# The attention mask of a pooling step: penalties gathered from a table by the sequence's type, one addition in place of four masked products

## The chip, the cores and the metric

The kernel runs on one core of one Trainium2 chip. The metric is device time in microseconds (us) of one execution. The core has TensorE (PE), VectorE (DVE), ScalarE (ACT), GpSimd (POOL) and the sync engine's queue (SP), which issues most of the DMAs.

## The reference, cut to what matters

Four residual layers are applied to `x` of 16 sequences x 256 positions x 256 channels, all in float32. Layer 0 has sixteen exponential moving averages and a layer norm. Layer 1 is the pooling that the change touches. Layer 2 is a mixture of eight experts and a shared one, computed for every sequence, and layer 3 a two-layer head whose last 64 output columns come from an expert chosen by the sequence.

```
attn_in = tanh(hidden @ W1 + b1);  scores = attn_in @ v            # one score for each key l
mask = where(pt == 0, l <= j, where(pt == 1, l >= j, l != j))      # pt: type of the sequence, 0, 1 or 2
p = softmax(where(mask, scores[:, None, :], -1e30), axis=-1)       # 256 rows j, 256 keys l
cnt = sum(mask, -1)
x = x + einsum('bjl,bld->bjd', p, hidden) / cnt[..., None]
```

The type is an input, one integer for each of the 16 sequences.

## The kernel before, in words

**Work.** The 16 sequences form eight blocks of two. Each sequence of a block is a lane `s` (0 or 1). Layers 0 and 1 of a lane are cut into 47 side steps (`side(b, s, j)`, j = 0 to 46). Layers 2 and 3 of a block are a run of experts, each in eight chunks. One expert chunk of a whole block is twelve matmuls of 512 columns (`front`), an activation on ACT, a product on DVE (`hid`), a split of the result into a rounded high part on ACT and a low remainder on POOL (`hid_lo`, in `late`), and six matmuls into `ps_out` (`back`). Each matmul product is written as three, of high and low parts. The weights of a chunk are split likewise by ACT (`w_hi`) and DVE (`w_lo`) in `cut`. After the last chunk of an expert DVE adds `ps_out` into `acc` with the expert's coefficient, and the next expert's first `back` waits for it.

**Order.** Each engine runs its own share of one list, `ORDER`, made by the planner `order()` before the kernel is built. The side steps of blocks 1 to 7 are dealt out between the fronts. `side_cost(b, j)` gives each step a cost, and the lane with the smaller sum of costs goes next, lane 1 having started 12 units behind. After each front `pace(i) * step_budget(i - 1)` is added to a credit (capped at 6), and side steps are placed while it is positive. `pace` is the cost still to be placed for a block, over the budget that is left before the block's first front, and at most 1.1. A step that uses PE isn't placed behind a front if its lane has already had a step of non-zero cost there. If a block is due and its side steps are not all placed, the rest are placed at once, back to back (here called a join). The cost function before:

```
if 7 <= j < 7 + ND:
    return 2.1
...
return {0: 1.3, 5: 1.0, 34: 1.7, 36: 1.4, 39: 2.1, 42: 1.5, 24: 0.0, ...}.get(j, 0.7)
```

Block 0 has a written order: lane 0's steps, with some of lane 1's between them, come before the first front.

**Steps touched by the change.** Steps 8 to 23 have the sums of the averages on POOL (`add1` to `add15`), which add `trace[s][d % 3]` to `temporal[s]`. The third buffer, `trace[s][2]`, is last used by `add14`. Step 24 does nothing before. Step 39: PE multiplies by `v` so that the scores, the same in every partition, stand in PSUM; DVE (lines 1031, 1034, 1038) adds the penalties to them: `mask[:, 0]` (keys after the row) times `pen[:, 0, q]`, `mask[:, 1]` (keys before the row) times `pen[:, 1, q]`, and for each half of the rows the identity `idn` times `pen[:, 2, q]` on the diagonal. `pen` holds -1e30 or 0 for each sequence. Step 40 is the row maximum (1042) and its negation. Step 41 has transposes of the layer's input on PE (617), which overwrite the bank of the scores and so wait for the first of the four products (`sc0`), and the exponentials on ACT (817). Step 42 is the division on DVE (1056), 44 the transposes of the probabilities on PE (626), 46 the product.

POOL also gathers expert rows with an indirect DMA (line 1213): 128 rows of 512 floats for each sequence. `setup("route")` on POOL works out `typ`, `pen`, `cnt`, the coefficients and the row numbers for that gather.

Of the kernel before, what the change touches and what calls it, by code (L numbers as in the profile page):

```python
# [5 lines left out]
P = 128  # L6
B, S, D = 16, 256, 256
T = B * S
DH = D // P
BB = 2  # L10
BT = BB * S
NBLK = T // BT
ND = 16
# [38 lines left out]
NEG = -1e30  # L52
# [31 lines left out]
def side_cost(b, j):  # L84

    if 7 <= j < 7 + ND:
        return 2.1
    if b == 0 and j in (1, 26, 30, 32, 45):
        return 0.0
    return {0: 1.3, 5: 1.0, 34: 1.7, 36: 1.4, 39: 2.1, 42: 1.5, 24: 0.0, 25: 0.0, 29: 0.0, 37: 0.0, 43: 0.0}.get(j, 0.7)  # L90

# [14 lines left out]
def order():  # L106
# [126 lines left out]
    while queue:  # L233
# [11 lines left out]
            + [f"{what}{d}" for d in range(ND) for what in ("mul", "scan")]  # L245
            + ["t_lo", "prod", "p_lo", "q_lo", "rstd", "norm", "affine", "x1", "sc0", "sc1", "score",
               "max", "top", "xT_lo", "den", "rden", "prob", "probT_lo", "res"])
# [22 lines left out]

def residual_stack_kernel(nc, xT, chunks, head_chunks, sidew, vec128, w64, masks, ident, we_rows,
                          be_pad, blendT, taus, types, experts, gates, shared_gate, yT):
# [5 lines left out]
    with ctx:  # L278
# [68 lines left out]
        bn2_half = sb("bn2_half", [ND, 1])  # L347
        mask = sb("mask", [P, 2, 2, S], bf16)
        idn = sb("idn", [P, P])
# [11 lines left out]
        typ = sb("typ", [P, 5, B])  # L361
        pen = sb("pen", [P, 3, B])
        cnt = sb("cnt", [P, B, 2])
        ge = sb("ge", [P, B, NE])
# [21 lines left out]
        s_x = [[sem(f"x_in{s}_{i}") for i in range(2)] for s in range(BB)]  # L386
        s_we = [sem(f"we_in{i}") for i in range(2 * BB)]
        s_y = [sem(f"y_out{i}") for i in range(NACC)]

# [47 lines left out]
        def _(sp):  # L437
# [33 lines left out]
            sp.dma_start(wa1_t[:].rearrange("p k a -> p (k a)"), sidew[:, NSPLIT:NSPLIT + 2 * P]).then_inc(s_late, 16)  # L471
            sp.dma_start(mask[:].rearrange("p n j l -> p (n j l)"), masks.bitcast(bf16)).then_inc(s_late, 16)
            sp.dma_start(idn[:], ident[:]).then_inc(s_late, 16)
# [22 lines left out]
        def _(pe):  # L496
# [26 lines left out]
            def side(b, s, j):  # L523
# [79 lines left out]
                elif j == 38:  # L603
                    pe.wait_ge(l_dve[s], dve_at(s, b, "x1"))
                    pe.wait_ge(l_act[s], act_at(s, b, "std"))
                    if b == 0:
                        pe.wait_ge(s_late, 64)
                    plain_sum(ps[:, 0:S], [(wa1_t[:, k, :], temporal[s][:, k, :])
                                             for k in range(DH)]).then_inc(l_pe[s], 1)
                elif j == 39:  # L610
                    pe.wait_ge(l_act[s], act_at(s, b, "attn"))
                    mm(ps[:, 0:S], v_col.broadcast_to([P, P]), sm[:], start=True, stop=True).then_inc(l_pe[s], 1)
                elif j == 41:
                    pe.wait_ge(l_dve[s], dve_at(s, b, "sc0"))
                    for lh in range(2):
                        for dh in range(DH):
                            last = nc.tensor.transpose(ps[:, lh * D + dh * P:lh * D + (dh + 1) * P],
                                                       temporal[s][:, dh, lh * P:(lh + 1) * P], idn[:])
                    last.then_inc(l_pe[s], 1)
                elif j == 44:  # L620
                    pe.wait_ge(l_dve[s], dve_at(s, b, "prob"))
                    if b == 0:
                        pe.wait_ge(l_act[s], act_at(s, b, "xT"))
                    for jh in range(2):
                        for lh in range(2):
                            last = nc.tensor.transpose(ps[:, lh * S + jh * P:lh * S + (jh + 1) * P],  # L626
                                                       trace[s][1][:, jh, lh * P:(lh + 1) * P], idn[:])
                    last.then_inc(l_pe[s], 1)
                elif j == 46:
                    if b == 0:  # L630
                        pe.wait_ge(l_act[s], act_at(s, b, "probT"))
                    else:
                        pe.wait_ge(l_dve[s], dve_at(s, b, "probT_lo"))
                    for dh in range(DH):
                        c = slice(dh * P, (dh + 1) * P)
                        if b == 0:
                            last = plain_sum(both[:, dh, :], [(gated[s][:, lh, c], soma[s][:, lh, :]) for lh in range(2)])
                        else:
                            last = exact_sum(both[:, dh, :], [(one_hi[s][:, lh, c], one_lo[s][:, lh, c],
                                                               two_hi[s][:, lh, :], two_lo[s][:, lh, :]) for lh in range(2)])  # L640
                    last.then_inc(l_pe[s], 1)
# [68 lines left out]
            for x in ORDER:  # L710
# [4 lines left out]
                elif x[0] == "back":  # L715
                    (back_plain if x[1] < NLONE else back)(x[1])
                elif x == ("setup", "bias"):
                    pe.wait_ge(su_pool, su(SETUP_POOL, "onehot"))
                    pe.wait_ge(s_late, 64)
                    mm(ps_out[:, 0, 0:B], be_sb, onehot[:], start=True, stop=True).then_inc(su_pe, 1)  # L720
# [184 lines left out]
        def _(dve):  # L905
# [39 lines left out]
            def side(b, s, j):  # L945
# [80 lines left out]
                elif j == 39:  # L1026
                    if b == 0:
                        dve.wait_ge(su_pool, su(SETUP_POOL, "onehot"))
                        dve.wait_ge(s_late, 64)
                    dve.wait_ge(l_pe[s], pe_at(s, b, "score"))  # L1030
                    STT(score[:], mask[:, 0], pen[:, 0, q:q + 1],
                        ps[:, 0:S].unsqueeze(1).broadcast_to([P, 2, S]), ALU.mult, ALU.add).then_inc(l_dve[s], 1)
                    mine("sc0")
                    STT(score[:], mask[:, 1], pen[:, 1, q:q + 1], score[:], ALU.mult, ALU.add).then_inc(l_dve[s], 1)
                    mine("sc1")
                    for jh in range(2):
                        diagonal = score[:, jh, jh * P:(jh + 1) * P]
                        last = STT(diagonal, idn[:], pen[:, 2, q:q + 1], diagonal, ALU.mult, ALU.add)
                    last.then_inc(l_dve[s], 1)
                elif j == 40:  # L1040
# [118 lines left out]
        def _(pool):  # L1159
# [6 lines left out]
            def setup(j):  # L1166
# [8 lines left out]
                elif j == "route":  # L1175
# [10 lines left out]
                    done("cnt0")  # L1186
                    TS(pen[:], typ[:, 1:4, :], NEG, None, ALU.mult)
                    for jh in range(2):
# [4 lines left out]
                    done("cnt1")  # L1193
                    TT(cnt[:], parts[:, 0], parts[:, 1], ALU.add)
                    TS(sg[:, 1, :], sg[:, 0, :], -1.0, 1.0, ALU.mult, ALU.add).then_inc(su_pool, 1)
                    done("sg")
                    TT(cnt[:], cnt[:], parts[:, 2], ALU.add)
                    for e in range(NE):
                        TT(coef[:, e, :], ge[:, :, e], sg[:, 1, :], ALU.mult)
# [17 lines left out]
            def side(b, s, j):  # L1217
                if 9 <= j < 8 + ND:
                    d = j - 8
# [103 lines left out]
```

## Time and profile before

| | |
|---|---|
| median of 3 runs | 2991.48 us (2990.12 to 2994.9) |
| profiled execution | 2992.09 us |
| its span, first to last instruction | 2990.3 us (1.8 us lie around it) |
| mean granted TensorE clock | 0.979 |
| busy: PE / DVE / ACT / POOL | 2856.0 / 1782.0 / 1425.4 / 1169.9 us |

The busy time is the sum of an engine's instructions in the profiled execution. PE works for 96% of the span, so what can be won by a change to another engine is in the rest: the stretches in which PE waits. The granted clock is 1.00 at 2.4 GHz and 0.50 at 1.2 GHz.

### The profile page before, as it was taken

To read this page: it belongs to the slowest core of one execution; us is meant where nothing else is said; L and a number is where in the kernel's file an instruction comes from. 1 tells how busy PE (TensorE), PEld (TensorE's weight loads), DVE (VectorE), ACT (ScalarE), POOL (GpSimd) and SP (SyncE) were. 2 spreads that over 40 slices of the span, in tenths; PEclk is the share of its full clock that TensorE was granted. 3 is DMA by queue.
4 is the path that set the end of the run, shared out by engine and by line. 5 is a ranking of instruction groups with operands and counts; after the bars stand their busy time and mean duration, and the time that the engine had idled before them with its cause. 6 is when DMAs were issued, how large, how long until landed. Compare 5 with 4: busy or idle time off the path is not lost.

```text
span 2990.3 us, 37374 instructions
## 1 busy us (share of the span) xinstructions
PE 2856.0 (96%) x13486; PEld 2384.0 (80%) x13486; DVE 1782.0 (60%) x2922; ACT 1425.4 (48%) x2460; POOL 1169.9 (39%) x931
## 2 busy tenths in 40 slices
PE   5799999998999999998999999999899998999998
PEld 3588788887888888887888878888788887888887
DVE  7668776765665576656665467656455555333443
ACT  1244664464345563455434555347533446334544
POOL 4216334533443245433454235543334433333333
PEclk6899999999999999999999999999999999999999
DMA  2223231121111131112111112112111112111331
GB/s 100 92 90 94 79 103 43 53 78 43 50 51 44 45 89 60 48 37 87 49 43 43 46 44 84 43 43 70 55 43 53 51 48 77 60 48 45 115 99 39
DMA packets 75688, 185.87 MB, mean 62 GB/s; under 512 B 8936, under 2 KB 21744, under 8 KB 75504
## 3 DMA queue, kind: packets, MB, share of 16 engines
q1 hardware_dynamic: 73648, 179.17, 19.7%
q0 software_dynamic: 1280, 4.20, 0.4%
q8 instruction: 108, 1.77, 0.2%
q14 instruction: 76, 0.62, 0.1%
q10 hardware_dynamic: 576, 0.11, 0.0%
HBM read 179.25 MB, written 4.19 MB: 61 GB/s over the span
## 4 chain that ended last, share of the span: by engine, by line
PE 85%; DVE 8%; ACT 3%; issue 3%; DMA 0%; POOL 0%; DVEq 0%; ACTq 0%; SPq 0%
PE bank L508 18%; PE bank L510 18%; PE bank L509 18%; PE ps_out L508 9%; PE ps_out L510 9%; PE ps_out L509 9%; PE bank L501 3%; DVE w_lo L1076 2%; DVE trace L990 2%; DVE trace L998 1%; PE bank L578 1%; ACT w_hi L835 1%; PE ps_out L663 1%; DVE acc L1122 1%; PE bank L626 0%
## 5 line engine op out<-in xcount | busy, mean ns | idle before, releaser
L1229 POOL TENSOR_TENSOR hid_lo<-hid,hid_hi 128x512 fp32r<-128x512 f32 (+1 forms) x640 | 825.1, 1290 | 1638.4 <-ACT hid_hi L882 1638.1
L508 PE MATMUL bank<-res_lo,w_hi 128*128 128x512 f32 (+1 forms) x2432 | 950.4, 391 | 6.7 <-issue 3.9
L509 PE MATMUL bank<-res_hi,w_lo 128*128 128x512 f32 (+1 forms) x2432 | 938.1, 386 | 0.0
L510 PE MATMUL bank<-res_hi,w_hi 128*128 128x512 f32 (+1 forms) x2432 | 937.9, 386 | 0.0
L1105 DVE TENSOR_TENSOR hid<-hid,bank 128x512 f32<-128x512 f32 (+1 forms) x608 | 397.0, 653 | 628.9 <-PE bank L510 513.0
L872 ACT ACTIVATE hid<-bank 128x512 f32<-128x512 f32 (+1 forms) x608 | 349.7, 575 | 743.6 <-PE bank L510 666.3
L1076 DVE TENSOR_TENSOR w_lo<-w_raw,w_hi 128x768 fp32r<-128x768 f32 (+1 forms) x488 | 441.6, 905 | 385.6 <-ACT w_hi L835 310.0
L510 PEld LDWEIGHTS bank<-res_hi,w_hi 128*128 128x128 f32 x2432 | 458.8, 189 | 97.1
L508 PEld LDWEIGHTS bank<-res_lo,w_hi 128*128 128x128 f32 x2432 | 459.7, 189 | 95.6 <-issue 8.4
L835 ACT ACTIVATE w_hi<-w_raw 128x768 fp32r<-128x768 f32 x360 | 304.3, 845 | 466.0 <-PE ps_out L510 465.8
L509 PEld LDWEIGHTS bank<-res_hi,w_lo 128*128 128x128 f32 x2432 | 459.8, 189 | 81.6
L508 PE MATMUL ps_out<-hid_lo,w_hi 128*128 128x512 f32 (+1 forms) x1344 | 504.8, 376 | 13.5 <-DVE acc L1122 12.8
L510 PE MATMUL ps_out<-hid_hi,w_hi 128*128 128x512 f32 (+1 forms) x1344 | 503.9, 375 | 0.0
L509 PE MATMUL ps_out<-hid_hi,w_lo 128*128 128x512 f32 (+1 forms) x1344 | 503.7, 375 | 0.0
L882 ACT ACTIVATE hid_hi<-hid 128x512 fp32r<-128x512 f32 (+1 forms) x640 | 391.9, 612 | 11.1 <-DVE hid L1105 10.8
L1223 POOL TENSOR_TENSOR temporal<-temporal,trace 128x512 f32<-128x512 f32 x240 | 327.5, 1365 | 151.0 <-DVE trace L998 150.9
L998 DVE TENSOR_TENSOR_SCAN trace<-bank,trace 128x256 f32<-128x256 f32 x480 | 304.8, 677 | 8.2
L508 PEld LDWEIGHTS ps_out<-hid_lo,w_hi 128*128 128x128 f32 x1344 | 253.3, 188 | 66.8 <-issue 16.7
L509 PEld LDWEIGHTS ps_out<-hid_hi,w_lo 128*128 128x128 f32 x1344 | 253.7, 189 | 46.9
L510 PEld LDWEIGHTS ps_out<-hid_hi,w_hi 128*128 128x128 f32 x1344 | 253.7, 189 | 45.3
L990 DVE SCALAR_TENSOR_TENSOR trace<-gated,bl,bank 128x256 f32<-128x256 f32 x512 | 221.6, 474 | 57.6 <-PE bank L578 52.1
L578 PE MATMUL bank<-mod_pair,sel 128*128 128x256 f32 x256 | 82.5, 328 | 43.3 <-DVE trace L998 17.6
(178 smaller groups left out, 1952.9 us busy)
## 6 DMA issues: line engine op xcount, KB each, us to landing
w_raw<-in_chunks SPq DMA_DIRECT2D x360, 384.0 KB, 3.0
w_raw<-in_head_chunks SPq DMA_DIRECT2D x64, 224.0 KB, 2.5
plain<-in_chunks SPq DMA_DIRECT2D x32, 384.0 KB, 3.2
x_in<-in_xT SPq DMA_DIRECT2D x16, 256.0 KB, 3.4
out_yT<-acc SPq DMA_DIRECT2D x8, 512.0 KB, 3.1
acc<-in_sidew SPq DMA_DIRECT2D x2, 512.0 KB, 7.0
acc<-in_sidew SPq DMA_DIRECT2D x1, 320.0 KB, 5.4
mask<-in_masks SPq DMA_DIRECT2D x1, 256.0 KB
```

The source lines that it names most:

```text
L508: mm(out, wh, xl, start=start and i == 0, stop=False, skip_group_check=not lone)
L509: mm(out, wl, xh, start=False, stop=False, skip_group_check=not lone)
L510: last = mm(out, wh, xh, start=False, stop=end, skip_group_check=not lone)
L835: last = activate(w_hi[k][:], raw[:], ACT.Copy)
L872: activate(h[:, tok], ps_gate[i % 2][:, tok], ACT.Silu).then_inc(s_act, 1)
L882: activate(hid_hi[i % DEPTH][:, tok], hid[i % 3][:, tok], ACT.Copy).then_inc(s_hhi, 1)
L990: last = STT(tr[:, h, :], gated[s][:, h, :], bl[:, h, d:d + 1], (lead_mix[d % 2] if lead else ps)[:, 0:S], ALU.mult, ALU.mult)
L998: last = V.tensor_tensor_scan((temporal[s] if d == 0 else tr)[:, h, :], decay.broadcast_to([P, S]), tr[:, h, :], 0.0, ALU.mult, ALU.add)
L1076: return TT(w_lo[k][:, cols], src, f(w_hi[k][:, cols]), ALU.subtract)
L1105: TT(h[:, tok], h[:, tok], ps_up[i % 2][:, tok], ALU.mult).then_inc(s_hid, 1)
L1223: nc.gpsimd.tensor_tensor(temporal[s][:], temporal[s][:], trace[s][d % 3][:], ALU.add).then_inc(l_pool[s], 1)
L1229: nc.gpsimd.tensor_tensor(hid_lo[i % DEPTH][:, tok], hid[i % 3][:, tok], f(hid_hi[i % DEPTH][:, tok]), ALU.subtract).then_inc(s_hlo, 1)
```

## The change

The host makes a table `penalties` of 384 rows of 512 floats. Row `128 * type + p` has, for the positions j that partition p holds (p and p + 128), 0 where the type allows a key and -1e30 where not. In step 24 POOL gathers the 128 rows of the sequence's type into `trace[s][2]`. In step 39 DVE adds that to the scores once. The bf16 masks and their load are gone. The planner's cost of step 39 falls from 2.1 to 0.7. PE's step 41 waits for the finished sum.

```
-    return {0: 1.3, 5: 1.0, 34: 1.7, 36: 1.4, 39: 2.1, 42: 1.5, 24: 0.0, ...}.get(j, 0.7)
+    return {0: 1.3, 5: 1.0, 34: 1.7, 36: 1.4, 42: 1.5, 24: 0.0, ...}.get(j, 0.7)
...
-            sp.dma_start(mask[:].rearrange("p n j l -> p (n j l)"), masks.bitcast(bf16)).then_inc(s_late, 16)
...
                 elif j == 41:
-                    pe.wait_ge(l_dve[s], dve_at(s, b, "sc0"))
+                    pe.wait_ge(l_dve[s], dve_at(s, b, "score"))
...
                 elif j == 39:
-                    if b == 0:
-                        dve.wait_ge(su_pool, su(SETUP_POOL, "onehot"))
-                        dve.wait_ge(s_late, 64)
+                    dve.wait_ge(s_pen[s], 16 * (b + 1))
                     dve.wait_ge(l_pe[s], pe_at(s, b, "score"))
-                    STT(score[:], mask[:, 0], pen[:, 0, q:q + 1],
-                        ps[:, 0:S].unsqueeze(1).broadcast_to([P, 2, S]), ALU.mult, ALU.add).then_inc(l_dve[s], 1)
-                    mine("sc0")
-                    STT(score[:], mask[:, 1], pen[:, 1, q:q + 1], score[:], ALU.mult, ALU.add).then_inc(l_dve[s], 1)
-                    mine("sc1")
-                    for jh in range(2):
-                        diagonal = score[:, jh, jh * P:(jh + 1) * P]
-                        last = STT(diagonal, idn[:], pen[:, 2, q:q + 1], diagonal, ALU.mult, ALU.add)
-                    last.then_inc(l_dve[s], 1)
+                    TT(score[:], trace[s][2][:], ps[:, 0:S].unsqueeze(1).broadcast_to([P, 2, S]),
+                       ALU.add).then_inc(l_dve[s], 1)
...
-                    TS(pen[:], typ[:, 1:4, :], NEG, None, ALU.mult)
+                    TS(pen[:, 0, :], typ[:, 2, :], float(P), row_id, ALU.mult, ALU.add)
+                    TS(pen[:, 1, :], typ[:, 3, :], 2.0 * P, None, ALU.mult)
...
+                    TT(pen[:, 2, :], pen[:, 0, :], pen[:, 1, :], ALU.add)
...
+                    G.tensor_copy(pen_row[:], pen[:, 2, :])
...
             def side(b, s, j):
-                if 9 <= j < 8 + ND:
+                if j == 24:
+                    if b == 0:
+                        done("onehot")
+                    pool.wait_ge(l_pool[s], pool_at(s, b, f"add{ND - 1}"))
+                    q = b * BB + s
+                    nc.gpsimd.indirect_dma_start(
+                        out=trace[s][2][:].rearrange("p j l -> p (j l)"), out_offset=None, in_=penalties[:],
+                        in_offset=bass.IndirectOffsetOnAxis(ap=pen_row[:, q:q + 1], axis=0)).then_inc(s_pen[s], 16)
```

PE's waits for the late loads go from 64 to 48, since there is one load less.

## Rows read from the trace of the kernel before

**Rows 1.** The page: span, and busy time of each engine.

```profile
span 2990.3 us, 37374 instructions
...
PE 2856.0 (96%) x13486; PEld 2384.0 (80%) x13486; DVE 1782.0 (60%) x2922; ACT 1425.4 (48%) x2460; POOL 1169.9 (39%) x931
```

**Rows 2.** The page: the chain that ended last, by engine.

```profile
PE 85%; DVE 8%; ACT 3%; issue 3%; DMA 0%; POOL 0%; DVEq 0%; ACTq 0%; SPq 0%
```

**Rows 3.** Waits of PE, whole span: total us, times, longest us.

```profile
PE bank L626 <- DVE trace L1056: 33.7, 11, 6.4
...
PE ps_out L508 <- DVE acc L1122: 12.8, 11, 2.4
```

**Rows 4.** Groups by form: xcount | busy us, mean ns of one | idle before.

```profile
L1038 DVE SCALAR_TENSOR_TENSOR trace<-idn,pen,trace 128x128 f32<-128x128 f32 x32 | 17.5, 588 | 0.6
...
L1034 DVE SCALAR_TENSOR_TENSOR trace<-mask,pen,trace 128x512 f32<-128x512 bf16 x16 | 12.9, 808 | 0.6
...
L1031 DVE SCALAR_TENSOR_TENSOR trace<-mask,pen,bank 128x512 f32<-128x512 bf16 x16 | 11.9, 743 | 8.0 <-PE bank L612 8.0
L1067 DVE TENSOR_TENSOR acc<-bank,temporal 128x512 f32<-128x512 f32 x16 | 11.0, 686 | 14.9 <-PE bank L510 12.1 <-PE bank L501 2.8
...
L1042 DVE TENSOR_REDUCE top<-trace 128x2 f32<-128x512 f32 x16 | 10.8, 675 | 0.1
```

**Rows 5.** The chain at three of the steps 39: start us, us, what.

```profile
77.47 0.76 DVE trace L1031
...
79.69 0.70 DVE top L1042
...
399.19 0.67 DVE trace L1031
...
402.19 0.60 DVE gated L978
...
1367.60 0.67 DVE trace L1031
...
1370.73 0.54 DVE w_lo L1076
```

**Rows 6.** PE's waits in 77:92, 165:172, 334:342, 404:414, 671:692, 1374:1380, 2084:2092.

```profile
PE bank L626 <- DVE trace L1056: 5.1, 1, 5.1
...
PE bank L578 <- DVE temporal L998: 2.0, 1, 2.0
...
PE ps_out L508 <- DVE acc L1122: 0.8, 1, 0.8
...
PE bank L626 <- DVE trace L1056: 2.6, 1, 2.6
...
PE bank L626 <- DVE trace L1056: 5.6, 1, 5.6
...
PE ps_out L508 <- DVE acc L1122: 2.3, 1, 2.3
...
PE ps_out L508 <- DVE acc L1122: 1.2, 1, 1.2
```

**Rows 7.** Three stretches: length, busy of each engine, granted clock, DMA share, GB/s.

```profile
399.00:417.00 18.00, 15.36 (x78) 13.10 (x77) 17.04 (x32) 10.99 (x19) 6.76 (x5) 0.91 0.29 88
670.00:694.00 24.00, 13.52 (x66) 11.49 (x65) 17.30 (x30) 9.96 (x16) 5.37 (x4) 0.79 0.17 49
1366.00:1382.00 16.00, 13.74 (x59) 11.34 (x58) 14.60 (x27) 10.63 (x24) 7.25 (x6) 0.89 0.39 118
```

**Rows 8.** The gather of line 1213: issue on POOL, and landing.

```profile
L1213 POOL DMA_INDIRECT we_in<-in_we_rows,ex_row x16: 945/958/1497, 120.6 to 2509.0; - x16
...
DMA to landing us min/median/max: 3.5/4.0/4.8
```

**Rows 9.** POOL's last addition of block 0, lane 0; who waited for POOL's `hid_lo` (1229).

```profile
52.36 1.27 POOL L1223 TENSOR_TENSOR temporal<-temporal,trace 128x512 f32<-128x512 f32 x1 [0.80 <-DVE trace L998]
...
  PE ps_out L508: 0.4, 1
```

More of the change, by code:

```diff
@@ L89, in side_cost @@
         return 0.0
-    return {0: 1.3, 5: 1.0, 34: 1.7, 36: 1.4, 39: 2.1, 42: 1.5, 24: 0.0, 25: 0.0, 29: 0.0, 37: 0.0, 43: 0.0}.get(j, 0.7)
+    return {0: 1.3, 5: 1.0, 34: 1.7, 36: 1.4, 42: 1.5, 24: 0.0, 25: 0.0, 29: 0.0, 37: 0.0, 43: 0.0}.get(j, 0.7)
 def step_budget(i):
@@ L245 @@
             + [f"{what}{d}" for d in range(ND) for what in ("mul", "scan")]
-            + ["t_lo", "prod", "p_lo", "q_lo", "rstd", "norm", "affine", "x1", "sc0", "sc1", "score",
+            + ["t_lo", "prod", "p_lo", "q_lo", "rstd", "norm", "affine", "x1", "score",
                "max", "top", "xT_lo", "den", "rden", "prob", "probT_lo", "res"])
@@ L268, with residual_stack_kernel @@
 SETUP_ACT = ["tau", "blexp0", "blexp1", "hi0", "hi4", "hi8"]
-def residual_stack_kernel(nc, xT, chunks, head_chunks, sidew, vec128, w64, masks, ident, we_rows,
+def residual_stack_kernel(nc, xT, chunks, head_chunks, sidew, vec128, w64, penalties, ident, we_rows,
                           be_pad, blendT, taus, types, experts, gates, shared_gate, yT):
@@ L347, in residual_stack_kernel @@
         bn2_half = sb("bn2_half", [ND, 1])
-        mask = sb("mask", [P, 2, 2, S], bf16)
         idn = sb("idn", [P, P])
@@ L362, in residual_stack_kernel @@
         pen = sb("pen", [P, 3, B])
+        pen_row = sb("pen_row", [P, B], u32)
         cnt = sb("cnt", [P, B, 2])
@@ L387, in residual_stack_kernel @@
         s_we = [sem(f"we_in{i}") for i in range(2 * BB)]
+        s_pen = [sem(f"penalty_in{s}") for s in range(BB)]
         s_y = [sem(f"y_out{i}") for i in range(NACC)]
@@ L606, in side @@
                     if b == 0:
-                        pe.wait_ge(s_late, 64)
+                        pe.wait_ge(s_late, 48)
                     plain_sum(ps[:, 0:S], [(wa1_t[:, k, :], temporal[s][:, k, :])
@@ L718, in _ @@
                     pe.wait_ge(su_pool, su(SETUP_POOL, "onehot"))
-                    pe.wait_ge(s_late, 64)
+                    pe.wait_ge(s_late, 48)
                     mm(ps_out[:, 0, 0:B], be_sb, onehot[:], start=True, stop=True).then_inc(su_pe, 1)
@@ L1217, in side @@
             def side(b, s, j):
-                if 9 <= j < 8 + ND:
+                if j == 24:
[6 more added lines that the diff above has]
+                        in_offset=bass.IndirectOffsetOnAxis(ap=pen_row[:, q:q + 1], axis=0)).then_inc(s_pen[s], 16)
+                elif 9 <= j < 8 + ND:
                     d = j - 8
@@ L1279 @@
     key = np.arange(S)
-    masks = np.stack([key > j[:, :, None], key < j[:, :, None]], 1).reshape(P, -1).astype(np.uint16) * 0x3F80
+    allowed = np.stack([key <= j[:, :, None], key >= j[:, :, None], key != j[:, :, None]])
+    penalties = np.where(allowed, 0.0, NEG).astype(f32).reshape(3 * P, -1)
     picks = np.zeros((P, ND), f32)
@@ L1301 @@
                                tall(g["L1_cond_b1"][:, None]), tall(g["L1_cond_v"][:, None])], 1),
-        "masks": masks,
+        "penalties": penalties,
         "ident": np.eye(P, dtype=f32),
```

## The prediction

> **What bounds the kernel now.** I read the page first. PE is busy for 2856.0 of 2990.3 us [rows 1]. The change gives PE no matmul less, so it can win only in the 134 us in which PE isn't busy, or by a higher clock. The chain that ended last says who holds PE up there: 85% is PE's own work, 8% DVE's, 3% ACT's, and POOL and the DMAs have none [rows 2]. DVE therefore matters, but only where it is late. The view of who waited for whom gives the places: the longest total is PE's wait for the probabilities (33.7 us in 11 waits), and another is its wait for the expert's sum in `acc` (12.8 us in 11) [rows 3]. None of them names step 39. So I listed the 16 times of step 39 and asked at each whether the chain runs through it, and which wait of PE ends behind it. It runs through seven of the sixteen. The other nine (from 610 to 2519 us) lie beside it, and what is cut there gives nothing.
>
> **What the change removes on DVE.** Lines 1031, 1034 and 1038 are busy for 11.9 + 12.9 + 17.5 = 42.3 us [rows 4]. In their place come 16 additions of 128x512 with one operand in PSUM and one in SBUF. The trace has that very shape in line 1067: 686 ns [rows 4]. 16 x 0.69 = 11.0 us, so DVE gets 31.3 us lighter. That is the most that the change can give; only the part on the chain counts.
>
> **Place by place.** In the chain the step reaches from the start of 1031 to the start of what follows [rows 5], and after the change it takes 0.69 + 0.02 of issue = 0.7 us.
> - 77 us, block 0, lane 0: 79.69 - 77.47 = 2.2 us, cut 1.5. Behind it the maximum, the exponentials and the division stand in a row, and PE waits 5.1 us for them [rows 6]: all 1.5 counts.
> - 165 us: the same length, so cut 1.5; PE's wait behind it is 2.0 [rows 6]: 1.5.
> - 334 us: the step is no shorter there, but the wait behind it is only 0.8 [rows 6]: 0.8.
> - 399 us: 402.19 - 399.19 = 3.0, cut 2.3; DVE is without a pause up to the wait of 2.6 [rows 6]: 2.3. DVE is busy for 17.04 of these 18 us [rows 7].
> - 671 us, a join: again 3.0 long, cut 2.3, in front of a wait of 5.6 [rows 6]: 2.3.
> - 1367 us: 1370.73 - 1367.60 = 3.1, cut 2.4, wait 2.3 for `acc` [rows 6]: 2.3.
> - 2084 us: 3.0 long, cut 2.3, wait 1.2 [rows 6]: 1.2.
>
> Sum 1.5 + 1.5 + 0.8 + 2.3 + 2.3 + 2.3 + 1.2 = 11.9 us. Where the stalls at 399 and 1367 go, nothing else is late next: PE's neighbouring matmuls have their operands.
>
> **The clock.** In the stretches with these two stalls the granted clock is 0.91 over 18 us and 0.89 over 16 us [rows 7], so part of each ran at 1.2 GHz behind the pause. At 1.00 they would give back up to 0.09 x 18 + 0.11 x 16 = 3.4 us. At 671 the pause stays long, and I take nothing for it. On the same point the Trainium skill (TensorE: Matmul & The Clock Gate, "What's actually happening") says that the throttled rate is the default and activity releases it. The falls behind the pauses agree (0.91, 0.89, 0.79). By a sum that leaves the clock out the gain would be 3.4 us smaller.
>
> **What the planner does with the lower cost.** Step 39 gets 1.4 units cheaper, so the credit left behind it is 1.4 higher, and step 40 can follow behind the same front where before it came one or more fronts later. Its maximum takes 0.68 us on DVE [rows 4]. At 399, 1367 and 2084 that work moves into the very stretch that gets relief: up to 3 x 0.68 = 2.0 us. From below this price is nothing, where the interleaving of the lanes puts another step first. Since `pace` is the cost still to be placed over the budget left, the total (about 2.8 units less of a block) is only spread thinner, and the end of a block's side work stays where it was. I take the full 2.0. Steps 41 to 46 stay in separate fronts by the lane rule, except in joins. Which steps meet at a cut or a closing sum of an expert is drawn anew, though: the noise of this I carry in the range.
>
> **What is added.** A gather of the same size as line 1213's: 128 rows of 2 KB. POOL: 0.96 us each, at most 1.5 [rows 8], with some 0.3 of issue around 1.3 us, 16 times, 20 us in all on an engine that is busy for 39% [rows 1]. It comes right behind `add15`. What queues behind it is the next `hid_lo`, for which PE waited only once in the whole span, 0.4 us [rows 9], as it is used three fronts later: 0 to 1.3 us each, I take nothing. If the cover were gone, it would be 16 x 1.3 = 21 us. The POOL setup has two small instructions and a copy more, under 1 us, before the first addition of step 9, whose buffer is needed three steps later: nothing. DMA: the gather lands 4.0 us after issue, at most 4.8 [rows 8]. The tightest place is block 0, lane 0: `add15` ends at 52.4 + 1.3 = 53.6 us [rows 9] and step 39 begins at 77.5 [rows 5], 23.9 us for at most 1.5 + 4.8 = 6.3. Later blocks have some ten fronts between steps 24 and 39. So DVE's new wait costs nothing. 16 x 256 KB more traffic, less one mask load of 256 KB behind all the early ones, meets DMA engines busy for 0.17 to 0.39 [rows 7]: nothing.
>
> A rule speaks against this part. The Trainium skill (SBUF — State Buffer, "SBUF: two separate sides") calls it a trap that VectorE can keep GpSimd from writing the descriptors of a DMA that it issues. In the trace the sixteen gathers are issued amid DVE work in 0.95 to 1.5 us [rows 8]. By the row the gather costs nothing. By the rule it comes late by some vector instructions, which the 17.6 us of margin hold too. So both leave the sum as it is, and only the rival below has it.
>
> **PE's new wait.** Step 41's transposes waited for the first product (0.74 us) and now wait for the sum (0.69 us): equal.
>
> **The sum.** 11.9 + 3.4 - 2.0 = 13.3 us. Against the profiled execution's own 2992.1 that is 2978.8. Its time is 0.6 above the median of the runs, so I predict 2978.2 us.
>
> **Rivals.**
> - *A join gets lighter too.* If the dealing puts the division one front earlier at a join, its wait of 5.6 us goes, and with it the clock loss of that stretch while PE is busy: 0.21 x 13.5 = 2.8 us [rows 6, 7]. With no price for step 40 the gain is 11.9 + 3.4 + 5.6 + 2.8 = 23.7: 2968 us. I count it into the faster side. It sets the lower end.
> - *The gain is eaten.* The chain passes DVE at seven places only, and steps that come forward fill them again, or another latency of ACT stands right behind. Then the places give 1.5 + 1.5 at the start and little after: within 6 us, about 2989. For it: DVE is busy for 17.04 of 18 us at 399 [rows 7]. Against it: what comes forward is 0.68 us, the cut 2.3.
> - *Slower, by closings.* The order drawn anew lets averages or head cuts on DVE stand before the closing sum at more places. One such place costs the wait of 2.3 and 0.11 x 16 = 1.8 of clock, 4.1 us [rows 6, 7]. From four new ones on the gain of 13.3 is gone; five give 2991.5 - 13.3 + 20.5 = 2999 us. Against it: of some 80 closings only 11 have this wait before [rows 3], and DVE is 31 us lighter.
> - *The gather is late.* Then DVE stands in step 39, with `hid` behind it and PE behind that. It decides from 24 us of delay in block 0: with 10 us beyond it, some 2989, and more if later blocks have it. Nothing near it is in the rows.
>
> **How the numbers follow.** The forecast with its lighter-join variant has 0.68, the gain eaten 0.19, slower by closings 0.10, the late gather 0.03. Two tenths of a per cent are 6 us, about what a measurement of this kernel tells from no change. Faster by more is 0.68, within 0.20 (the eaten gain and a little of the gather), slower 0.12. The range runs from the lighter join, 2967, to no change, 2991: left out are the slower cases and a little below, two in ten.
>
> **What would show it.** In the profile after: one group of 16 DVE additions near 690 ns in place of three groups; DVE near 1751 us; PE's busy time unchanged or slightly lower by clock, its waits down by about 10 us; the 2.3 and 1.2 us waits for `acc` at 1376 and 2089 gone; the wait for the probabilities near 79 us 3.6 in place of 5.1; 16 more indirect DMAs with no wait of DVE behind them. The prediction is wrong if the waits of PE for probabilities or `acc` turn up in new places as large as those removed, or if DVE waits for the gather.

## The result, and the profile after

| | before | after |
|---|---|---|
| median | 2990.46 us (6 runs, 2989.09 to 2994.9) | 2974.66 us (6 runs, 2973.48 to 2977.36) |
| ratio after/before, 95% interval | | 0.9944 [0.9933, 0.9956] |
| profiled execution, its span | 2992.1, 2990.3 | 2973.48, 2971.7 |
| mean granted clock | 0.979 | 0.982 |

The kernel is 0.56% faster, some 16 us. The forecast was 2978.2 us with a range of 2967 to 2991: direction and size are right. Whether its steps are right is another question, and most of what follows is about that.

The page of the changed kernel: span and busy times, and the chain that ended last.

```profile
span 2971.7 us, 37357 instructions
...
PE 2847.9 (96%) x13486; PEld 2378.2 (80%) x13486; DVE 1754.1 (59%) x2874; ACT 1420.7 (48%) x2457; POOL 1184.5 (40%) x950
...
PE 88%; DVE 6%; ACT 3%; issue 2%; DMA 0%; POOL 0%; ACTq 0%; DVEq 0%; SPq 0%
```

Against [rows 1, 2]: PE is busy 8 us less with the same matmuls (clock), DVE 27.9 us less, POOL 14.6 us more, and DVE's share of the chain went from 8% to 6%. The groups by form of the changed kernel (xcount | busy us, mean ns | idle before), with the sum that served as the price of the new addition:

```profile
L1058 DVE TENSOR_TENSOR acc<-bank,temporal 128x512 f32<-128x512 f32 x16 | 11.0, 686 | 14.1 <-PE bank L510 12.1 <-PE bank L501 2.1
L1029 DVE TENSOR_TENSOR trace<-trace,bank 128x512 f32<-128x512 f32 x16 | 10.9, 684 | 8.4 <-PE bank L612 8.4
```

The waits of PE over the whole span of the changed kernel (total us, times, longest):

```profile
PE bank L626 <- DVE trace L1047: 26.8, 7, 6.4
...
PE bank L508 <- DVE two_lo L1051: 11.9, 5, 4.6
PE ps_out L508 <- DVE acc L1113: 11.1, 10, 2.6
```

The wait for the probabilities fell from 33.7 us in 11 to 26.8 us in 7, the one for `acc` only from 12.8 to 11.1 [rows 3]. The page says where time is left, not where it was won. For that I took the start of ACT's `hid` of each expert front in both traces (the same 672 fronts of work in the same sequence) and subtracted. The columns are before minus the kernel named, in us; the places of step 39 are those of the prediction.

| up to front | time before | what lies in between | after | addition, old order (run 1 below) | four products, new order (run 2 below) |
|---|---|---|---|---|---|
| 0 | 93 | the place at 77 | 5.1 | 3.2 | 0.1 |
| 24 | 191 | the place at 165 | 10.4 | 7.6 | 3.7 |
| 104 | 515 | the places at 334 and 399 | 20.0 | 7.5 | 10.7 |
| 248 | 1151 | the join at 671 | 17.1 | 8.1 | 7.1 |
| 312 | 1442 | the place at 1367 | 19.7 | 9.7 | 6.6 |
| 440 | 2003 | | 21.9 | 8.2 | 8.8 |
| 472 | 2153 | the place at 2084 | 19.2 | 10.0 | 4.7 |
| 664 | 2963 | the rest | 18.6 | 9.9 | 4.1 |

Three readings. The changed kernel has won all its time by 515 us, and the remaining five sixths of the span give nothing net. It wins 9 us more than the same code in the old order of steps. And the nothing net is made of two parts: what the new order had won by itself shrinks from 10.7 to 4.1 us behind front 104, while the distance between the changed kernel and the four products in the same order grows from 9.3 to 14.5.

A column compares one execution of each kernel, so single values carry chance. At DVE's line 971, ahead of any changed code on that engine, the profiled executions of all twelve kernels stand between 12.2 and 14.1 us; before is at 13.61, the changed kernel at 12.21. So 1.4 of its first 5.1 us are probably no effect.

### The profile page after: what moved, and what is told of

Read it like the earlier page. It is cut to its first block, busy times and chain, and to the rows that moved or that the text cites. A ratio compares the mean times of both kernels' runs of the same rounds, so it can differ in the third digit from the quotient of the medians.

```text
span 2971.7 us, 37357 instructions
## 1 busy us (share of the span) xinstructions
PE 2847.9 (96%) x13486; PEld 2378.2 (80%) x13486; DVE 1754.1 (59%) x2874; ACT 1420.7 (48%) x2457; POOL 1184.5 (40%) x950
## 3 DMA queue, kind: packets, MB, share of 16 engines
q1 hardware_dynamic: 73504, 178.91, 19.2%
## 4 chain that ended last, share of the span: by engine, by line
PE 88%; DVE 6%; ACT 3%; issue 2%; DMA 0%; POOL 0%; ACTq 0%; DVEq 0%; SPq 0%
PE bank L508 19%; PE bank L510 19%; PE bank L509 19%; PE ps_out L508 9%; PE ps_out L510 9%; PE ps_out L509 9%; PE bank L501 3%; DVE trace L990 1%; DVE w_lo L1067 1%; PE bank L578 1%; DVE trace L998 1%; ACT w_hi L835 1%; PE ps_out L663 1%; DVE acc L1113 0%; ACT L817 0%
## 5 line engine op out<-in xcount | busy, mean ns | idle before, releaser
L508 PE MATMUL ps_out<-hid_lo,w_hi 128*128 128x512 f32 (+1 forms) x1344 | 504.2, 375 | 12.0 <-DVE acc L1113 11.1
L1113 DVE SCALAR_TENSOR_TENSOR acc<-ps_out,coef,acc 128x512 f32<-128x512 f32 x144 | 101.6, 745 | 27.5 <-PE ps_out L510 27.5
```

Source lines behind the costliest of these rows:

```text
L508: mm(out, wh, xl, start=start and i == 0, stop=False, skip_group_check=not lone)
```

## The experiments

Ten kernels, each timed in five rounds beside the kernel before.

**1. The addition without the new order.** The changed kernel, but the planner's old cost for step 39, so the sequence of steps is that of before.

```diff
-    return {0: 1.3, 5: 1.0, 34: 1.7, 36: 1.4, 42: 1.5, ...}.get(j, 0.7)
+    return {0: 1.3, 5: 1.0, 34: 1.7, 36: 1.4, 39: 2.1, 42: 1.5, ...}.get(j, 0.7)
```

> The changed kernel with the planner's cost of step 39 put back to 2.1, so that the order of the list is that of the kernel before. Theory A, the shorter step on DVE does it (the prediction's): the seven places give 11.9 us and up to 3.4 of clock, with nothing lost to step 40, so a ratio of 0.9949 to 0.996, 2975 to 2979 us. The waits for acc near 1376 and 2089 us are gone. Rival B, the order drawn anew carries most of the 16 us: then this one stays within 6 us of the kernel before, a ratio over 0.998.

Measured: 2982.53 us against 2991.88, ratio 0.9969 [0.9957, 0.9981], so 9.3 us. That is between the two theories: less than the seven places were to give, more than the rival left. This kernel makes the cut of each place readable, since everything else stands where it stood. At 399 us only half a microsecond came of 2.3 us. DVE's order of time around that step, before (start us, us, what, idle before it and its releaser):

```profile
398.23 0.96 DVE L1076 TENSOR_TENSOR w_lo<-w_raw,w_hi 128x768 fp32r<-128x768 f32 x1 [1.54 <-ACT w_hi L835]
399.10 0.74 DVE L1031 SCALAR_TENSOR_TENSOR trace<-mask,pen,bank 128x512 f32<-128x512 bf16 x1
...
403.32 0.95 DVE L1076 TENSOR_TENSOR w_lo<-w_raw,w_hi 128x768 fp32r<-128x768 f32 x1
```

and the same stretch of this run:

```profile
391.21 0.96 DVE L1067 TENSOR_TENSOR w_lo<-w_raw,w_hi 128x768 fp32r<-128x768 f32 x1 [1.54 <-ACT w_hi L835]
392.08 0.68 DVE L1029 TENSOR_TENSOR trace<-trace,bank 128x512 f32<-128x512 f32 x1
...
395.76 0.96 DVE L1067 TENSOR_TENSOR w_lo<-w_raw,w_hi 128x768 fp32r<-128x768 f32 x1 [1.54 <-ACT w_hi L835]
```

Before, the two `w_lo` are 5.09 us apart and DVE never pauses between them; now they are 4.55 apart, and 1.54 us of that is a new pause. ACT's rows say why. Before:

```profile
397.35 0.84 ACT L835 ACTIVATE w_hi<-w_raw 128x768 fp32r<-128x768 f32 x1 [1.68 <-PE ps_out L510]
...
401.90 0.85 ACT L835 ACTIVATE w_hi<-w_raw 128x768 fp32r<-128x768 f32 x1 [1.68 <-PE ps_out L510]
```

and in this run:

```profile
390.33 0.84 ACT L835 ACTIVATE w_hi<-w_raw 128x768 fp32r<-128x768 f32 x1 [1.68 <-PE ps_out L510]
...
394.89 0.85 ACT L835 ACTIVATE w_hi<-w_raw 128x768 fp32r<-128x768 f32 x1 [1.68 <-PE ps_out L510]
```

4.55 and 4.56 us apart: `w_hi` waits for PE, and PE goes at its own pace. DVE had been half a microsecond behind that pace, so half a microsecond is what could be cut. The fronts show just that: 7.0 us of lead before this place, 7.5 behind it. The clock stayed as it was: 0.91 in the 18 us around this step, as in [rows 7].

```profile
391.50:409.50 18.00, 15.72 (x80) 13.51 (x79) 15.25 (x29) 10.99 (x19) 6.51 (x5) 0.91 0.30 85
```

The two other large places, as PE's waits of this run, first in 655:690, then in 1360:1400:

```profile
PE bank L626 <- DVE trace L1047: 5.6, 1, 5.6
PE bank L508 <- DVE two_lo L1051: 2.9, 1, 2.9
PE bank L578 <- DVE temporal L998: 0.8, 1, 0.8
...
PE bank L508 <- DVE two_lo L1051: 3.6, 1, 3.6
PE bank L626 <- DVE trace L1047: 2.7, 1, 2.7
PE ps_out L508 <- DVE acc L1113: 1.9, 1, 1.9
```

At the join the 5.6 us [rows 6] stand unchanged; only a smaller wait in front of it gave, 2.1 us before and 0.8 now. Its DVE rows are the picture of 399 again. The first `w_lo` of the join starts at 663.31, and the one behind step 39 has a pause that it did not have before:

```profile
666.54 1.06 DVE L1067 TENSOR_TENSOR w_lo<-w_raw,w_hi 128x768 fp32r<-128x768 f32 x1 [0.98 <-ACT w_hi L835]
```

The two are 3.23 us apart, and were 4.60 apart (670.80 and 675.40): 1.4 us of the 2.3 arrived, one went into waiting for `w_hi`. Of the 1.4 the fronts keep 0.6. At 1367 the `acc` wait shrank by 0.4 of 2.3.

At 334 us the prediction's 0.8 us came. PE's `acc` wait of 0.8 us [rows 6] is gone, and the lead goes from 7.6 to 8.6 us. Between there and 399 the lead falls to 7.0, because in this execution the clock dropped once behind that place. The same twelve microseconds of work, in the kernel before and in this run:

```profile
349.00:361.00 12.00, 10.26 (x56) 8.44 (x55) 8.16 (x13) 7.41 (x14) 3.74 (x3) 1.00 0.24 66
```
```profile
341.00:353.00 12.00, 10.26 (x46) 8.31 (x45) 8.07 (x13) 6.31 (x12) 3.05 (x3) 0.86 0.24 66
```

**2. The new order without the addition.** The kernel before, with the planner told that step 39 costs 0.7.

```diff
-    return {0: 1.3, 5: 1.0, 34: 1.7, 36: 1.4, 39: 2.1, 42: 1.5, ...}.get(j, 0.7)
+    return {0: 1.3, 5: 1.0, 34: 1.7, 36: 1.4, 42: 1.5, ...}.get(j, 0.7)
```

> The kernel before with its four masked products and no gather, only the planner's cost of step 39 lowered to 0.7, so that the list's order is that of the changed kernel. Theory A: step 40's maximum comes forward into stretches where DVE is late, 0 to 2 us slower, and the rest is noise of the new order: ratio 0.999 to 1.002. Rival B: 0.996 or less.

Measured: 2986.42 us, ratio 0.9982 [0.9973, 0.9991], 5.4 us faster, which neither theory had (0.999 and more, 0.996 and less). So a wrong cost in the planner makes the old code faster. Its fronts gain 3.7 us by front 24: PE's waits in 144:180 are 3.2 us before and 0.6 here. By front 104 the order is 10.7 us ahead, and 4.1 at the end. Together the first two runs account for 0.31% + 0.18% = 0.49% of the 0.56%, within the intervals.

Run 2 is also the partner of the changed kernel: the same order, four products against one addition. By the ratios (0.9944 over 0.9982) the addition is worth 11.4 us there, where it was worth 9.3 in the old order.

**3 and 4. The gather: none, and two.** In run 3 the addition takes a tile of zeros and no row is gathered, which leaves the mask out of the computation. In run 4 each gather is issued twice, the second waiting on POOL for the first.

```diff
-                    dve.wait_ge(s_pen[s], 16 * (b + 1))
-                    TT(score[:], trace[s][2][:], ...
+                    TT(score[:], fixed[:], ...
```
```diff
+                    for n in range(2):
+                        if n:
+                            pool.wait_ge(s_pen[s], 32 * b + 16)
                         nc.gpsimd.indirect_dma_start(...).then_inc(s_pen[s], 16)
```

> The changed kernel without the sixteen gathers: the addition takes a tile of zeros, set once on POOL at the start, so the mask is left out of the result. The order is the changed kernel's. Theory A, the gather is hidden (1.3 us of POOL each, right behind the last sum): equal to the changed kernel within 1.5 us, ratio to the kernel before 0.9939 to 0.995. Rival C, POOL's time or the contention costs up to 1.3 us each, 21 us in all: 2954 us, ratio 0.988.

> The changed kernel with each gather issued twice, the second when the first has landed, so that POOL stands for some 4 us of landing and 1.3 us of issue more at each of the sixteen places, about 6.6 us in all from the last sum to the next split. Theory A: hid_lo is used three fronts later, some 11 us, so PE waits little: at most 0.5 us a place, within 8 us of the changed kernel. Rival C: what POOL loses is seen one for one, 16 x 5 = 80 us slower, ratio 1.02.

Measured: 2975.37 us, ratio 0.9945 [0.9931, 0.9958], without; 2977.51 us, ratio 0.9955 [0.9941, 0.9968], with two. Without is the changed kernel again, 0.9944. The gathers of the changed kernel on POOL, with the landing:

```profile
L1219 POOL DMA_INDIRECT trace<-in_penalties,pen_row x16: 955/963/1507, 53.2 to 2444.4; - x16
...
DMA to landing us min/median/max: 3.2/3.4/4.5
```

and what run 4's POOL stood idle for:

```profile
  DMA trace<-in_penalties,pen_row: 46.6, 16
```

Sixteen stops of 2.9 us each, plus sixteen more issues of 0.95, hold up POOL for 62 us in all and cost the kernel some 3 us, with intervals that overlap. The one gather of the changed kernel is hidden with room to spare.

**5 and 6. Side work that ends earlier.** The joins keep waits that step 39 cannot shorten (5.9 + 2.9 us in 655:676 of the changed kernel). Both kernels with more reserve in the planner's `pace`:

```diff
-                most = max(most, need[STEPS[k][1]] / max(1.0, given - 8.0))
+                most = max(most, need[STEPS[k][1]] / max(1.0, given - 24.0))
```

> The changed kernel with a planner that aims to finish a block's side steps 24 budget units before its first front in place of 8, so that at the joins of blocks 2, 6 and 7 steps 41 to 46 stand between fronts. Theory D, what is left in DVE's shadow is at the joins: the waits there in the changed kernel's trace, 5.9 + 2.9, 6.4 + 2.9 and 5.1 + 1.4 us, go, 24.5 us, and with them some 5 us of halved clock, so 2945 to 2951 us, ratio 0.985 to 0.987. Rival E, the denser packing in front of each block makes DVE late for acc and the averages instead: at most 8 us gained, ratio over 0.9915.

> The kernel before (four masked products) with the same earlier finish. Theory D: 25 to 30 us gained, ratio 0.990 to 0.992, and the changed kernel's lead over it in the same order of steps shrinks to what the shorter step gives by itself, 8 to 12 us. Rival E: ratio over 0.997.

Measured: the changed kernel with it 2951.8 us against 2992.29, ratio 0.9868 [0.9853, 0.9884]; the kernel before with it 2965.84, ratio 0.9914 [0.9901, 0.9928]. The first beats both kernels, by 40 and some 23 us (forecast 2945 to 2951 us; the ratio lies in its range). PE's waits over the span of that run:

```profile
PE bank L626 <- DVE trace L1047: 13.2, 4, 4.6
...
PE bank L508 <- DVE two_lo L1051: 2.6, 2, 2.0
```

26.8 us became 13.2, and 11.9 became 2.6. The joins of the changed kernel held 5.9 + 2.9, 6.4 + 2.9 and 5.1 + 1.4 us of these. The stretch with the first join, in the changed kernel and in this run (length; busy of PE, PEld, DVE, ACT, POOL; granted clock; DMA share; GB/s):

```profile
600.00:720.00 120.00, 106.64 (x548) 90.63 (x547) 71.14 (x129) 68.91 (x133) 39.07 (x30) 0.96 0.21 65
```
```profile
600.00:720.00 120.00, 115.24 (x588) 98.22 (x587) 76.58 (x137) 78.13 (x141) 43.38 (x33) 0.99 0.24 69
```

Forty matmuls more in the same 120 us, at 0.99 in place of 0.96. Of the 24.4 us between the two profiled spans, 7.5 are PE's busy time (2847.9 to 2840.4 us at a mean clock of 0.982 and 0.987), the rest are waits. And the change itself is worth 14.0 us between the two kernels with the early finish, nearly its 15.8 without: what it gives doesn't hang on the joins. The forecast had said that this lead would shrink to 8 to 12 us, and it did not.

**7. The addition in block 0 only**, in the old order; the other fourteen steps 39 keep the four products.

```diff
+                    if b:
+                        STT(score[:], mask[:, 0], ...   # the four products as before
+                        ...
+                        return
                     TT(score[:], trace[s][2][:], ...
```

> The order of the kernel before. Block 0's two lanes have the gathered penalties and one addition, blocks 1 to 7 the four masked products. Theory F, from the trace of the one-addition kernel in the old order: 7.6 us of its gain are there by the 32nd front, so this one gains nearly as much as that, 7 to 9 us, ratio 0.997 to 0.9977. Rival, the prediction's places: block 0 gives only 1.5 + 1.5 = 3 us, ratio 0.999.

Measured: 2984.12 us, ratio 0.9977 [0.9968, 0.9986], 6.9 us by the ratio. Of run 1's 9.3 us, block 0's two places have about three quarters, with intervals of 2.7 and 3.6 us on either side of the two figures. The eleven executions of this one kernel go from 2982.9 to 2989.3 us, and they go with their mean granted clock: 2982.9 to 2985.9 us at 0.981 and 0.982, 2987.8 to 2989.3 at 0.979 and 0.980. The profiled one is of the latter (2988.53), and its fronts are only 3.9 us ahead at front 32, where run 1's, with the same work up to there, are 7.6 ahead. So the clock's chance in block 0 is as large as the places themselves.

**8. Half the discount.** The changed kernel with `39: 1.4` in the table of costs.

> The changed kernel with the planner's cost of step 39 at 1.4, between the old 2.1 and the new 0.7: another order, the same instructions. Theory G, the 5 us that the order gives are the luck of which steps meet: this one falls anywhere from 2972 to 2985 us, and need not lie between the two. Rival H, a lower cost is better by a mechanism: 2975 to 2982, between them.

Measured: 2977.18 us, ratio 0.9948 [0.9934, 0.9962]. Half of the lower cost brings nearly all of the new order's gain: 2.5 us short of the changed kernel, not told apart from it. Both theories allow this value.

**9. The addition in block 0, lane 0 only**, in the old order: the condition of run 7 is `if b or s:`.

> The kernel before with its order of steps; only step 39 of block 0, lane 0 (at 77 us) uses the gathered addition, the other fifteen keep the four products. By the prediction's step for this place the cut is 1.5 us: first expert's `hid` near 93.3 us in place of 94.8, time near 2990, ratio 0.9995. Rival, the clock: the 1.5 us also move the stretch at half rate, so that it ends near 85 us in place of 92.5 and the last matmuls of the lead run at the higher level: first `hid` near 90.7 us, a gain of about 4 us, ratio near 0.9987. The difference lies inside the interval of the ratio, so the profile's row of the granted clock in 84 to 92 us decides: 0.50 by the first, 0.6 and above by the second.

Measured: 2988.19 us, ratio 0.9985 [0.9976, 0.9994], 4.5 us; the 1.5 us of the prediction (0.9995) lie outside the interval, if barely. The rows show where more can come from. Before, the windows 84:88, 88:92 and 92:96, then ACT's first `hid`:

```profile
84.00:88.00 4.00, 3.05 (x9) 2.49 (x10) 2.47 (x6) 0.60 (x1) 0.01 (x1) 0.50 0.00 0
88.00:92.00 4.00, 3.13 (x8) 1.99 (x8) 0.78 (x2) 0.00 (x0) 1.26 (x1) 0.50 0.00 0
92.00:96.00 4.00, 4.00 (x15) 3.31 (x14) 1.21 (x3) 0.69 (x3) 0.00 (x0) 0.68 0.00 0
```
```profile
93.02 0.39 ACT L872 ACTIVATE hid<-bank 128x256 f32<-128x256 f32 x1 [6.79 <-PE bank L501]
95.70 0.38 ACT L872 ACTIVATE hid<-bank 128x256 f32<-128x256 f32 x1 [2.30 <-PE bank L501]
```

and in this run:

```profile
84.00:88.00 4.00, 3.53 (x10) 2.52 (x8) 2.14 (x4) 0.60 (x1) 1.27 (x1) 0.50 0.00 0
88.00:92.00 4.00, 3.12 (x15) 2.36 (x14) 1.23 (x3) 0.38 (x1) 0.00 (x0) 0.94 0.00 0
```
```profile
90.53 0.38 ACT L875 ACTIVATE hid<-bank 128x256 f32<-128x256 f32 x1 [5.85 <-PE bank L504]
92.37 0.38 ACT L875 ACTIVATE hid<-bank 128x256 f32<-128x256 f32 x1 [1.46 <-PE bank L504]
```

Before, PE runs at 0.50, which is its 1.2 GHz, through the first two windows, and the 0.68 of the third puts the clock's return at 94.5 us, not at the 92.5 that I had read. With 1.5 us cut, the 0.94 puts it at 88.5. That is later than the 85 that I had expected, but it still comes in time for the first expert's matmuls: fifteen of them in 88:92 in place of eight. Step 39 starts at the same time in both traces (77.47 and 77.42 us); the two fronts are 2.49 and 3.33 us ahead, so the clock added 1.8 us to the 1.5 of the cut. It doesn't keep them: in 96:100 this run is at 0.84, the kernel before at 1.00, and by the fourth front the lead is 1.6 us. The changed kernel has 0.88 and 1.00 in 84:88 and 88:92 and its fronts at 87.89 and 89.73.

Run 6 shows that it is the earlier arrival that does this, and not the addition. It has the four products, but the execution that was profiled came to step 39 at 75.69 us, 1.8 ahead of the kernel before, with the same instructions in the same order up to there, so by chance. Its maximum of step 40 starts at 77.91, run 9's at 78.14, and its window 88:92 and first fronts are nearly run 9's:

```profile
88.00:92.00 4.00, 3.12 (x15) 2.57 (x15) 1.47 (x4) 0.38 (x1) 0.00 (x0) 0.88 0.00 0
```
```profile
90.29 0.38 ACT L872 ACTIVATE hid<-bank 128x256 f32<-128x256 f32 x1 [5.85 <-PE bank L501]
92.13 0.38 ACT L872 ACTIVATE hid<-bank 128x256 f32<-128x256 f32 x1 [1.46 <-PE bank L501]
```

In runs 1 and 3 to 10 the clock is back before 89.1 us, in the kernel before and in run 2 at 94.5 and 94.2. How much of the 4.5 us is the clock in an average execution isn't shown: the eleven go from 2983.7 to 2989.4 us, and the profiled one is the slowest of them.

**10. A still earlier finish**, `given - 40.0` in place of run 5's 24.

> The changed kernel with each block's side work due 40 budget units ahead of its experts' first use, where the run before this had 24 and the changed kernel has 8. Theory D (what the earlier finish gives is the removal of the waits at the joins): nothing is left at the joins for more reserve to remove, and the denser side work costs a little: 2952 us plus 0 to 8, ratio 0.987 to 0.990. Rival: the density never mattered, and looser ends everywhere go on giving: below 2946 us, ratio under 0.985.

Measured: 2950.51 us, ratio 0.9863 [0.9847, 0.9878]; beside run 5's 0.9868 no difference. The probability waits are down from 13.2 to 8.7 us in all, and the time doesn't show it; DVE is busy 6 us longer (1775.3 against 1768.9), but that this takes the gain back isn't shown. The value is just under the forecast's 0.987 to 0.990 and above the rival's 0.985, so the rival is out, and the denser side work costs nothing that can be measured.

## Why the prediction was right, and where it was not

The total was within 4 us, but the terms were not; errors of opposite sign cancelled, and that is luck.

**Bound, place of the gain: right.** PE bounds the kernel, and DVE's 31 us could count only where it is late: the additions alone gave 9.3 us of it in the old order (run 1), 11.4 in the new (changed kernel against run 2) and 14.0 with the early finish, the planner's cost included (run 5 against run 6).

**The price of the addition: right.** 16 x 684 ns, forecast 686. DVE's busy time is 1754.1, forecast near 1751. The new form has one operand from SBUF, and its sixteen times lie between 675 and 690 ns. The removed products with both from SBUF were another matter. The mean of 808 ns [rows 4] is fifteen times 752 and once 1644, and of the 32 products on the diagonal 24 took 339 to 352 ns and eight 1259 to 1382 (min/median/max in ns of lines 1038 and 1034, then the two rows of the 1644):

```profile
L1038 DVE SCALAR_TENSOR_TENSOR trace<-idn,pen,trace x32: 339/352/1382, 79.0 to 2521.9; 128x128 f32<-128x128 f32 x32
L1034 DVE SCALAR_TENSOR_TENSOR trace<-mask,pen,trace x16: 751/752/1644, 78.3 to 2520.0; 128x512 f32<-128x512 bf16 x16
...
2084.93 1.29 POOL L1229 TENSOR_TENSOR hid_lo<-hid,hid_hi 128x512 fp32r<-128x512 f32 x1 [1.38 <-ACT hid_hi L882]
2085.13 1.64 DVE L1034 SCALAR_TENSOR_TENSOR trace<-mask,pen,trace 128x512 f32<-128x512 bf16 x1
```

All nine long ones began while POOL was inside one of its own additions or subtractions (`hid_lo`, 1229, or a sum, 1223) and ended 0.1 to 0.6 us behind its end; where POOL was idle, none was long. That is why the step is 3.0 us long at 399, 671, 1367 and 2084 and 2.2 at 77, and it makes up 8.6 of the 42.3 us. The Trainium skill (SBUF — State Buffer, "SBUF: two separate sides") says that a VectorE operation with two SBUF inputs and a GpSimd operation that reads SBUF shut each other out, for the whole instruction of whichever starts first; the rows agree with that. For the form with one operand from PSUM there is the product `hid` (1105, 128x512), which was begun beside a running POOL instruction 438 times in the trace before and never took more than 690 ns.

**The places.** With the order held, by the fronts: the old order (kernel before against run 1) and the new one (run 2 against the changed kernel).

| place | forecast | old order | new order |
|---|---|---|---|
| 77 and 165 | 1.5 + 1.5 | 7.6 (3.2 by the first front) | 6.7 (5.0 by the first front) |
| 334 and 399 | 0.8 + 2.3, clock 1.6 | 1.0 + 0.5, less 1.6 by the clock | 0.6 + 2.0 |
| 671 | 2.3 | 0.6 | 0.7 |
| 1367 | 2.3, clock 1.8 | 1.6, given back by front 384 | 3.1 |
| 2084 | 1.2 | 1.9 | 1.4 |

The new order's column adds up to 14.5 us where the ratios give 11.4, as its two profiled executions are the slowest of run 2 and the quickest of the changed kernel. In it, the places behind block 0 came to about two thirds of their forecast of 12.3 us with the clock; in the old order to less than a quarter.

- The two places in block 0 were sized too low. The step "PE waits 5.1 us for them: all 1.5 counts" was right as far as it went (the wait is 3.7 now), but the clock term was looked for only where PE paused in 399:417 and 1366:1382, not in the lead, where PE runs at 0.50 for the longest stretch of all. That was worth 1.8 us at the second front of run 9's execution. How much of the 7.6 us is the cut and how much the clock's chance isn't separated: run 7's execution has 3.9 at the same front for the same work. Of the 2.4 us that the second lane adds (run 7 less run 9), 1.5 was forecast, well inside the intervals; run 1's waits in 144:180 fell from 3.2 to 2.0 us.
- The step that failed at 399 in the old order is "DVE is without a pause up to the wait of 2.6: 2.3", with "nothing else is late next". DVE busy for 17.04 of 18 us [rows 7] reads as a bound, but it says only that DVE has no pause, not that it is far behind. ACT's `w_hi`, itself waiting for PE, was 0.5 us ahead of DVE and came every 4.55 us whatever DVE did. The chain of waits names the last to arrive, and the one just ahead of it is not in it. The prediction had this as a rival ("another latency of ACT stands right behind") at 0.19. In the new order it is much the same: the two `w_lo` around the step are 5.40 us apart in run 2 and 4.56 in the changed kernel, with a pause of 0.59 us for `w_hi`, so 0.8 us arrived. The rest of the 2.0 is the clock, below.
- The clock term of 3.4 us was nothing in the old order: 0.91 and 0.89 stand in run 1 where [rows 7] have them. In the new order it came at 399, in some executions. The 18 us around this step in run 2, in the changed kernel and in run 3, which has the changed kernel's order and additions and only no gather:

```profile
394.00:412.00 18.00, 14.96 (x81) 13.14 (x80) 15.09 (x27) 11.10 (x20) 6.13 (x5) 0.91 0.22 67
...
386.00:404.00 18.00, 15.62 (x93) 13.23 (x92) 14.95 (x27) 12.04 (x21) 6.42 (x6) 1.00 0.24 70
...
388.00:406.00 18.00, 15.79 (x85) 13.60 (x85) 13.82 (x25) 10.83 (x21) 6.52 (x5) 0.91 0.28 85
```

- At the join in the old order the same again: `w_hi` took one of the 2.3 us, and the 5.6 us wait was not shortened by what stands in front of the maximum: PE came to it earlier too. In the new order the wait is 7.4 us in run 2 and 5.9 in the changed kernel.

**The planner: wrong in sign.** The step was "I take the full 2.0" as a price, since step 40's maximum would crowd DVE at 399, 1367 and 2084. It does move as said: in the changed kernel the maximum stands directly behind the addition (388.98 us). But the order drawn anew is worth 5 us (run 2; 7.5 by the ratios of the changed kernel and run 1). PE's pauses in 144:180 are part of it (3.2 us before, 0.6 in run 2). I had put the redrawn order into the range, as noise, and it was the second largest term. That the order alone gains is shown; why this sequence is better is shown only by that place, and why half the discount does as well stays open. The full clock at 399 is not the order's, as run 2 has 0.91 there.

**The sum against the ratio.** 9.3 of run 1 + 5.4 of run 2 = 14.7 us of 16 to 17, with about 2 us that the two make together or that is noise.

**The gather, the table's traffic, PE's new wait at step 41: right.** Run 3 has no gather and the same time. DVE waited for it nowhere, and PE for the sum once (0.6 us). The rule of the Trainium skill that I weighed against it (SBUF — State Buffer, "SBUF: two separate sides": VectorE can keep GpSimd from writing descriptors) would have made it late by some instructions. The rows show none of that: issue took 955 to 1507 ns amid DVE work and landing at most 4.5 us, as the row of the older gather had said [rows 8].

**The rivals.** The lighter join did not come: the 5.6 us wait is 5.9. It took run 5's reserve to remove it. "Slower, by closings" was half right as a mechanism, and it is the order that does it: of the two `acc` waits that were to go, the 2.3 at 1376 fell to 0.2, but one of 1.5 us stands at 2070, in run 2 as well. And in place of two waits of 2.9 and 3.1 us from 1393 us on, run 2 and then the changed kernel have these, in 1354:1400 and 1354:1382:

```profile
PE bank L508 <- DVE two_lo L1060: 5.6, 1, 5.6
PE bank L626 <- DVE trace L1056: 3.1, 1, 3.1
PE ps_out L508 <- DVE acc L1122: 1.2, 1, 1.2
```
```profile
PE bank L508 <- DVE two_lo L1051: 4.6, 1, 4.6
PE bank L626 <- DVE trace L1047: 3.1, 1, 3.1
```

So the new order brings the larger waits, and the addition takes 1.0 us off each of two of them. That is why the last five sixths give nothing net: the addition goes on giving in the new order (9.3 to 14.5 us in the fronts) while the order's own lead melts from 10.7 to 4.1. In the old order the fourteen steps 39 there give 2.4 us (run 1 less run 7). By the prediction's own sign it isn't wrong: the waits for probabilities and `acc` fell by 8.6 us together, while those for `two_lo` rose by less, from 10.2 to 11.9.

## What to carry to other kernels

When a step on a busy engine is shortened, look for the second to arrive: take the next instruction that waits for anything else, and see in that releaser's own rows how far behind it the engine stood. At 399 us and at the join the cut was worth that distance, not its length. Where a planner deals out the work by costs, a change of a cost is a change of the whole order, to be measured alone as run 2 does; and its reserve is worth trying first, since here one constant gave 26 us on the old kernel and 23 on the new, more than the change to the arithmetic.

## What the runs showed of the hardware

In the lead, where PE runs at 0.50, arriving 1.6 to 1.8 us earlier at step 40 brought the clock back some 6 us earlier (88.5 and 89.0 us in place of 94.5) and put the first two fronts 2.5 to 2.7 and 3.3 to 3.6 us forward, in run 9 by the shorter step and in run 6 with the four products. The Trainium skill (TensorE: Matmul & The Clock Gate, "What's actually happening") says that the throttled rate is the default and activity releases it; the rows agree, as the release came earlier where PE's work came earlier. Part of the lead is lost again at the next fall of the clock.

A pause alone doesn't tell whether the clock falls: PE waited 2.6 us for the probabilities at 399 before, 3.0 in run 2, 2.3 in run 1, and 2.2 in the changed kernel and in run 3 alike, and the 18 us around it are at 0.91, 0.91, 0.91, 1.00 and 0.91. Executions of one kernel differ in their clock and their time together: the six of run 1 go from 2977.7 us at a mean clock of 0.983 to 2988.4 at 0.977.

A DVE instruction of the removed kind, with two operands from SBUF, that began while POOL was inside an elementwise instruction waited for its end, 345 ns becoming up to 1382 and 752 becoming 1644; with one operand from PSUM none did.
